# The start of a recurrent kernel: which transfers come first, what TensorE does until they land, and where weight casts and setup stand on VectorE

## What is computed

```python
def step(prev_h, xw_t):
    next_h = jnp.tanh(prev_h @ Wh + xw_t)
    return (next_h, next_h)
...
for e in range(E):
    we = jnp.sum(weights * (indices == e), axis=-1)
    h = jax.nn.silu(x2 @ W1[e].T + b1[e]) * (x2 @ W3[e].T + b3[e])
    y = y + (h @ W2[e].T + b2[e]) * we[:, None]
```

## Time and profile before

| | us |
|---|---|
| median of 3 runs | 152.13 |
| lowest and highest run | 150.54, 154.54 |
| the profiled execution: its own time | 150.08 |
| the profiled execution: its span | 148.3 |
| TensorE busy in the span | 140.9 (95%) |
| VectorE busy | 106.2 (72%) |
| ScalarE busy | 82.7 (56%) |
| GpSimd busy | 32.8 (22%) |

### The profile page before, as it was taken

How to read it: one execution, slowest core, us unless ns; L and a number is a source line. 1 busy time by engine, 2 the same in 40 slices (tenths; PEclk the granted TensorE clock), 3 DMA queues, 4 the chain that set the end, 5 groups by cost and what they waited for, 6 DMA issues and landing times.

```text
span 148.3 us, 3567 instructions
## 1 busy us (share of the span) xinstructions
PE 140.9 (95%) x1126; PEld 131.8 (89%) x1131; DVE 106.2 (72%) x400; ACT 82.7 (56%) x277; POOL 32.8 (22%) x86
## 2 busy tenths in 40 slices
PE   6499999999999999999989999999999999999993
PEld 1368899999899999999979999999999987999892
DVE  4008967698679168645989854999985799969851
ACT  3012247578567337554556554559878812856982
POOL 3003329621469123000016000003321000401100
PEclk9999999999999999999999999999999999999999
DMA  2999200000743000029300009700004910000011
GB/s 50 329 403 396 106 4 0 0 4 13 279 166 119 4 2 0 4 75 343 155 0 4 2 4 290 277 3 0 0 4 144 401 48 0 4 0 18 7 53 53
DMA packets 6834, 13.96 MB, mean 94 GB/s; under 512 B 1600, under 2 KB 3360, under 8 KB 6432
## 3 DMA queue, kind: packets, MB, share of 16 engines
q1 hardware_dynamic: 6384, 13.61, 25.4%
q10 hardware_dynamic: 432, 0.14, 0.4%
HBM read 13.15 MB, written 0.59 MB: 93 GB/s over the span
## 4 chain that ended last, share of the span: by engine, by line
PE 71%; DMA 12%; DVE 10%; issue 4%; ACTq 1%; ACT 1%; DVEq 1%
PE a L1056 15%; PE b L1056 13%; PE y_ps L1167 12%; PE rnn L1099 7%; PE y_ps L1068 6%; DVE hid L986 6%; DMA we_bc<-we_dram 5%; DMA wh_sb<-Wh 4%; DMA we_dram<-weT 3%; PE y_ps L1072 3%; PE b L1167 3%; PE m_ps L1099 2%; DVE hid L977 2%; PE a L1194 2%; PE rnn L1173 1%
## 5 line engine op out<-in xcount | busy, mean ns | idle before, releaser
L977 DVE SCALAR_TENSOR_TENSOR hid<-b,b_sb,gate_u 128x256 f32<-128x256 f32 (+1 forms) x80 | 33.6, 427 | 14.4 <-PE b L1056 10.7
L747 ACT ACTIVATE hs<-rnn 128x8 f32<-128x8 f32 x112 | 19.9, 178 | 33.4 <-PE rnn L1099 31.4
L1099 PEld LDWEIGHTS rnn<-hs,wh_sb 128*128 128x128 f32 x224 | 34.8, 191 | 0.7
L771 ACT ACTIVATE gate_u<-a,b_sb 128x256 f32<-128x256 f32 (+1 forms) x80 | 33.3, 427 | 1.9 <-DVE hid L977 1.0
L1099 PE MATMUL rnn<-hs,wh_sb 128*128 128x8 f32 x224 | 32.6, 218 | 0.0
L1167 PE MATMUL y_ps<-hid,w_sb 128*128 128x128 f32 (+1 forms) x160 | 32.3, 322 | 0.1
L986 DVE TENSOR_TENSOR hid<-hid,we_bc 128x128 f32<-128x128 f32 (+1 forms) x80 | 24.9, 352 | 3.1 <-DMA we_bc<-we_dram 3.1
L1167 PEld LDWEIGHTS y_ps<-hid,w_sb 128*128 128x128 f32 x160 | 24.3, 191 | 1.1
L1056 PE MATMUL a<-hs_hi,w_lo 128*128 128x256 f32 x48 | 16.2, 338 | 0.0
L1056 PE MATMUL a<-hs_hi,w_hi 128*128 128x256 f32 x48 | 15.3, 319 | 0.0
L1056 PE MATMUL a<-hs_lo,w_hi 128*128 128x256 f32 x48 | 15.0, 314 | 0.0
(11 more groups left out here) (152 smaller groups left out, 269.3 us busy)
## 6 DMA issues: line engine op xcount, KB each, us to landing
we_bc<-we_dram SPq DMA_DIRECT2D x12, 512.0 KB, 5.4
we_bc<-we_dram SPq DMA_DIRECT2D x8, 256.0 KB, 3.8
w_sb<-W1T SPq DMA_DIRECT2D x1, 1024.0 KB, 7.3
w_sb<-W3T SPq DMA_DIRECT2D x1, 1024.0 KB, 9.6
w_sb<-W2T SPq DMA_DIRECT2D x1, 1024.0 KB, 7.5
out<-out_sb SPq DMA_DIRECT2D x8, 64.0 KB, 1.5
xT_sb<-xT SPq DMA_DIRECT2D x1, 448.0 KB, 5.2
f_sb<-F1T SPq DMA_DIRECT2D x1, 256.0 KB, 6.9
```

The source lines that it names most:

```text
L747: act.activation(hs[:, cols], rnn_bank(n * BATCH, BATCH), ACT.Tanh).then_inc(h_ready, 1)
L771: act.activation(gate_u[:, n % U_RING, 0:w], a_ps[n % 2][:, 0:w], ACT.Silu, bias=b1_sb[:, e:e + 1]).then_inc(silu_ready, 1)
L977: dve.scalar_tensor_tensor(out=hid[:, n % H_RING, 0:w], in0=b_ps[n % 2][:, 0:w], scalar=b3_sb[:, e:e + 1], in1=gate_u[:, n % U_RING, 0:w], ...
L1099: pe.matmul(rnn_bank(n * BATCH, BATCH), wh_sb[:], prev, start=False, stop=True, skip_group_check=True).then_inc(z_ready, 1)
```

## The change

It does four things.

1. Transfers. The first tile of x moves from the SP queue to the head of ScalarE's queue, `Wh` from the third place there to the second on SP. The bias is loaded as one row of 512 bytes, not as 128 copies of it, and its product contracts over one partition with a row of ones. It is done before the wait for x and `Wx`.
2. TensorE's start. Six wide products of zeros stand ahead of the first wait in place of three, the twelve WARM products between the first steps are gone, and KEEPs of 256 columns may stand there. The one-column bias product moves from behind step 3 to the start.
3. VectorE. The casts may begin only behind step 22 and the setup only behind step 26.
4. The constants of the timetable: assumed landing times, slips, the order in which engines are asked, and `LIFT`. These change the order everywhere.

```diff
-START_KEEPS = 3
-WARM_STEPS = 6
+START_KEEPS = 6
+SPLITS_FROM, SETUP_FROM = 22, 26
...
-RNN_START = 4.7
-PE_SLIP, ACT_SLIP, KEEP_SLIP, MARGIN = 0.3, 0, 0.08, 0.14
+RNN_START = 5.0
+PE_SLIP, ACT_SLIP, KEEP_SLIP, MARGIN = 0.27, 0, 0.09, 0.13
...
-    for kind, t in (("X_IN", 7.2), ("MOE_IN", 12.3), ("L1_IN", 15.4), ("DOWN_IN", 18.0), ("START", RNN_START)):
+    for kind, t in (("SEEDS", 4.8), ("X_IN", 8.0), ("MOE_IN", 12.5), ("L1_IN", 18.0), ("DOWN_IN", 21.0), ("START", RNN_START)):
         put("DMA", kind, 0, 0.0, t)
     for b in range(2):
-        put("DVE", "SEED", b, 0.61, 0.75, [("BIAS", 0)])
+        put("DVE", "SEED", b, 0.61, 0.75, [("SEEDS", 0)])
     quarters = EXPERTS * P // BANK
     for q in range(quarters):
-        put("DVE", "W3_HI", q, 0.34, 0.48, [("MOE_IN", 0)], same("W3_HI", q))
-        put("DVE", "W1_HI", q, 0.34, 0.48, [("MOE_IN", 0)], same("W1_HI", q))
+        put("DVE", "W3_HI", q, 0.34, 0.48, [("MOE_IN", 0)], same("W3_HI", q) + [("TANH", SPLITS_FROM)])
+        put("DVE", "W1_HI", q, 0.34, 0.48, [("MOE_IN", 0)], same("W1_HI", q) + [("TANH", SPLITS_FROM)])
...
-        after = [("SETUP", d - 1)] if d else [("L1_IN", 0)]
+        after = [("SETUP", d - 1)] if d else [("L1_IN", 0), ("TANH", SETUP_FROM)]
...
-            sp.dma_start(xT_sb[:, 0:P], xT[:, 0:P]).then_inc(xw_in, 16)
             sp.dma_start(wx_sb[:], Wx).then_inc(xw_in, 16)
+            sp.dma_start(wh_sb[:], Wh).then_inc(rnn_in, 16)
             sp.dma_start(xT_sb[:, P:TOKENS], xT[:, P:TOKENS]).then_inc(x_in, 16)
...
-            act.dma_start(bh_bc[:], bh.broadcast_to([P, P])).then_inc(xw_in, 16)
+            act.dma_start(xT_sb[:, 0:P], xT[:, 0:P]).then_inc(xw_in, 16)
+            act.dma_start(bh_row[:], bh).then_inc(bias_row_in, 16)
             act.dma_start(h0_sb[:], h0T).then_inc(rnn_in, 16)
-            act.dma_start(wh_sb[:], Wh).then_inc(rnn_in, 16)
...
-            pe.wait_ge(xw_in, 48)
-            pe.wait_ge(row_ready, 1)
+            pe.wait_ge(ones_ready, 1)
+            pe.wait_ge(bias_row_in, 16)
+            pe.matmul(a_ps[0][:, 0:1], bh_row[:], ones_row[:, 0:1], start=True, stop=True, skip_group_check=True).then_inc(marked, 1)
+            pe.matmul(rnn_bank(0, P), bh_row[:], ones_row[:], start=True, stop=False, skip_group_check=True)
+            pe.wait_ge(xw_in, 32)
             rnn_inputs(0)
-            pe.matmul(rnn_bank(0, P), bh_bc[:], first_row[:], start=False, stop=False, skip_group_check=True)
```

More of the change, by code:

```diff
@@ L176, in run @@
         ready = dict.fromkeys(self.ops, 0.0)
-        engines = ("PE", "ACT", "DVE", "POOL", "SP", "DMA")
+        engines = ("PE", "ACT", "POOL", "DVE", "SP", "DMA")
         able = {e: [] for e in engines}
@@ L186, in run @@
         table, rnn_on = "silu", True
-        port, warm = 0.0, False
+        port = 0.0
         a_next, a_free, silu_end = 0, math.inf, {}
@@ L230, in run @@
                     y_idle = y_free is not None and y_free <= t
-                    if e == "PE" and warm and (y_idle or a_next < JOBS and a_free <= t) and (hot is None or t + LOAD < hot + KEEP_SLIP):
+                    if e == "PE" and (y_idle or a_next < JOBS and a_free <= t) and (hot is None or t + LOAD < hot + KEEP_SLIP):
                         orders[e].append(("KEEP", holds) if y_idle else ("KEEP_A", a_next))
@@ L287, in build_orders @@
     same = lambda kind, n: [(kind, n - 1)] if n else []
-    for kind, t in (("X_IN", 7.2), ("MOE_IN", 12.3), ("L1_IN", 15.4), ("DOWN_IN", 18.0), ("START", RNN_START)):
+    for kind, t in (("SEEDS", 4.8), ("X_IN", 8.0), ("MOE_IN", 12.5), ("L1_IN", 18.0), ("DOWN_IN", 21.0), ("START", RNN_START)):
         put("DMA", kind, 0, 0.0, t)
     for b in range(2):
-        put("DVE", "SEED", b, 0.61, 0.75, [("BIAS", 0)])
+        put("DVE", "SEED", b, 0.61, 0.75, [("SEEDS", 0)])
     quarters = EXPERTS * P // BANK
     for q in range(quarters):
-        put("DVE", "W3_HI", q, 0.34, 0.48, [("MOE_IN", 0)], same("W3_HI", q))
-        put("DVE", "W1_HI", q, 0.34, 0.48, [("MOE_IN", 0)], same("W1_HI", q))
+        put("DVE", "W3_HI", q, 0.34, 0.48, [("MOE_IN", 0)], same("W3_HI", q) + [("TANH", SPLITS_FROM)])
+        put("DVE", "W1_HI", q, 0.34, 0.48, [("MOE_IN", 0)], same("W1_HI", q) + [("TANH", SPLITS_FROM)])
         put("DVE", "W1_LO", q, 0.60, 0.74, [("W1_HI", q)], same("W1_LO", q))
         put("POOL", "W3_LO", q, 1.23, 1.37, [("W3_HI", q)], same("W3_LO", q))
-    put("PE", "BIAS", 0, [(LOAD, 0.007)] * 2, RESULT, [], [("RNN", WARM_STEPS // 2)])
-    for k in range(2 * WARM_STEPS):
-        put("PE", "WARM", k, [(LOAD, 0.213)], RESULT, [], [("RNN", k // 2)] + same("WARM", k))
     for t in range(STEPS):
         behind = same("RNN", t)
-        if 0 < t <= WARM_STEPS:
-            behind.append(("WARM", 2 * t - 1))
         if t and t % STEPS_PER_TILE == 0:
@@ L472, in adaln_ffn @@
         wx_sb, wh_sb = sb("wx_sb", [P, P]), sb("wh_sb", [P, P])
-        bh_bc, first_row = sb("bh_bc", [P, P]), sb("first_row", [P, P])
+        bh_row, ones_row = sb("bh_row", [1, P]), sb("ones_row", [1, P])
         hs = sb("hs", [P, TOKENS])
@@ L820, in link @@
                 dve.wait_ge(chain, links[0])
[L823 to L825 removed]
+            dve.memset(ones_row[:], 1.0).then_inc(ones_ready, 1)
             for t in (gmax, g_take):
@@ L992, in _ @@
                         dve.wait_ge(x_in, 16)
-                        dve.wait_ge(xw_in, 48)
+                        dve.wait_ge(xw_in, 32)
                     dve.wait_ge(y_done, (n + 1) * EXPERTS)
@@ L1042, in rnn_inputs @@
             def rnn_inputs(i):
-                pe.matmul(rnn_bank(i * P, P), wx_sb[:], xT_sb[:, tile_cols(i)], start=(i == 0), stop=False,
+                pe.matmul(rnn_bank(i * P, P), wx_sb[:], xT_sb[:, tile_cols(i)], start=False, stop=False,
                           skip_group_check=True)
@@ L1078, in _ @@
                 keep_wide()
-            pe.wait_ge(xw_in, 48)
-            pe.wait_ge(row_ready, 1)
+            pe.wait_ge(ones_ready, 1)
[3 more added lines that the diff above has]
+            pe.wait_ge(xw_in, 32)
             rnn_inputs(0)
-            pe.matmul(rnn_bank(0, P), bh_bc[:], first_row[:], start=False, stop=False, skip_group_check=True)
             for kind, n in ORDERS["PE"]:
-                if kind == "WARM":
-                    keep_wide()
-                if kind == "BIAS":
-                    pe.matmul(a_ps[0][:, 0:1], bh_bc[:], first_row[:, 0:1], start=True, stop=True, skip_group_check=True).then_inc(marked, 1)
                 if kind == "XIN":
```

12 lines of the change are left out of this document (4 added, 8 removed), and 8 rows, old and new, of the table LIFT.

## The result

The changed kernel took 145.91 us (median of four executions, 145.71 to 146.02). The kernel before took 153.13 us (four executions, 150.54 to 154.54). The ratio is 0.964, with a 95% interval from 0.955 to 0.973: 3.6% faster. The profiled executions are 145.98 and 150.08 us, with spans of 144.2 and 148.3.

What follows compares the result with a forecast made beforehand. It took TensorE's queued work, and when that may begin with the recurrence, as the bound. Start -2.3, middle -0.3 and tail +0.5 made -2.1 us, from the median 152.13 to 150.0 us, range 147.6 to 152.4.

Steps and rivals of the forecast that it cites:

- the casts fit beside the `hid`: VectorE, 20 to 53 us: 28.0 of 33 us busy, one cast of 0.36 us a step beside one `hid`.
- the tail costs 0.5 us more: Behind step 64: four fewer passes of A and B done by the last step, at 0.127 us each, +0.5 us.
- The wait of 39.80: Weighting at 39.19 waited 0.94 us for weights, TensorE stood 0.32; to go, with the slow copy at 26.04, for -0.7.
- one collision with a subtraction: VectorE's copy of `dT` at 26.04 took 1.22 us beside a GpSimd subtraction; to go, one new wait of +0.4 expected.
- -0.3 forecast for steps 16 to 64: Middle stretch: two old waits go, -0.7, and one new wait beside GpSimd's subtractions comes, +0.4.
- the casts stop the experts: VectorE, steps 22 to 46: each cast takes 0.89 us and delays a `hid`, 3.9 us lost, 153.5 us; chance 0.1.
- The clock: TensorE's start: rise at 6.9 us, only step 0 at the low level, 1.7 of 2.0 lost us come back.
- the first rival: TensorE's start: clock rises by 5.5, step 0 at 5.7, step 16 at 16.3, total -3.5, 148.6 us; chance 0.32.
- a rival: TensorE's start: clock rises late, four steps at about 1.1 us, sum -0.6 to -0.1, about 151.7 us; chance 0.18.
- My -2.3 for the start: Start to step 16: step 0 at 6.5 us and an earlier clock rise put step 16 at 17.3, not 19.6.
- The landing: First transfers: `Wh` lands at 5.56 us, `h0` at 6.1 with bounds 6.1 to 7.0; step 0 gains 0.6 us.
- The distance to the median: Whole kernel: the profiled 150.08 lay 2.05 us under the median 152.13; this distance was carried over to the changed kernel.

Runs made afterwards that it cites:

- the eight profiles: Profiles of the change, its variants and the kernel before with the new start, all with six wide products and early transfers; tanh of step 16 at 16.9 to 20.5 us.
- the run with ten zeros: Kernel before with the new start, plus ten narrow products of zeros between the inputs and step 0: 152.22 us, ratio 1.011.

## Why the prediction was off

**Right.** The end is set by when TensorE's full stretch begins; the casts fit beside the `hid` (0.41 us, one 0.71); the tail costs 0.5 us more. The wait of 39.80 went, because the weights are asked for 9 us earlier, and one collision with a subtraction went and another came: -0.3 forecast for steps 16 to 64, -0.6 measured. The slower rival, "the casts stop the experts", is refuted by VectorE at 28.34 of 33 us with TensorE at 32.91.

**The clock, by 0.6 us.** The step that failed was "with the 5.6 us that the rise took before, it comes at 6.9". It was there before 5.1 in the first profile. That took 0.4 off the products ahead of step 0 and the 0.2 of a step at the lower level, and with the landing below step 16 began at 16.47, not 17.3. That is nearer to the first rival (16.3; span 3.5 us less forecast, 4.1 measured). But no value was right for all: four of the eight profiles have the rise before 5.5, the others between about 10 and 13. I read a duration off one execution and used it as a property of the kernel. The Trainium skill's sentence on its variation stood in my text, and I gave it to a rival instead of to the width of my own case. My -2.3 for the start lies near the average difference of 2.2, and that is luck: no profile has the rise where I put it.

**The landing, by 0.2 us.** I put `Wh` at 5.56 and `h0` at 6.1. `Wh` landed at 3.8 (1.16 and 2.6), `h0` at 5.8. Both bounds of `h0` were too late in this execution; in others it landed up to 1.3 us later, at 7.2, beyond my upper bound of 7.0. I took `h0`'s time from its own place in the queue; it follows the big transfer of x, as the last section shows.

**Steps 64 to 127, -0.9 us.** I had no term there. The wait was to be seen at 74.74, and I had looked no further than step 64. It comes and goes with the landing of one chunk's weights.

**The distance to the median, 2.1 us.** This is the largest. I carried over the 2.05 us by which the profiled execution lay under the median, as if it were a constant of the program. For the changed kernel it is -0.07 in the first timing (145.98 profiled, median 145.91) and 1.4 us the other way in the second (149.79 profiled, median 148.39). The profile that I had read, of 150.08 us, was faster than any of the four timed executions, with step 16 at 20.0 where two later profiles of that start have 22.1: a rise that comes late makes 2.1 us by itself. The wait at 39.19, which I priced at the 0.32 us of one execution, can cost 15, but none of the four executions that make the 153.13 is over 154.54, so such a loss is in none of them. How much of the 2.1 each of the two gave stays open. Term by term: 0.8 (start) + 0.3 (16 to 64) + 0.9 (64 to 127) make the 2.0 us between the forecast span of 146.2 and 144.2, and 2.1 more make the 4.1.

**Luck in the measurement.** The four executions of the first timing lie within 0.3 us of each other and of the profiled one, which had the early rise; that all four had it is likely and not shown. The second timing gave 148.39, which is 1.6 us below the forecast and inside the range. There the forecast would have looked right, with the same wrong steps in it.

## What to carry to other kernels

A wait of TensorE in the middle of a full stretch is not worth only its length: it is a chance for the clock to fall. So look first at the other engine's queue: move the instruction that waits for a late operand further back, so that nothing that TensorE needs stands behind it. If the runs of a kernel spread by several per cent, ask which wait makes the long ones before you carry the distance from profile to median over to a change. A gain that hangs on the clock's rise at the start has to be timed more than once, and profiled more than once: here the two medians were 145.9 and 148.4, and the single times behind the second 146.1 to 149.8. Before you explain a loss by the edit you made, look for the stretch in which it stands: the run with ten zeros at the start lost its time near 94 us.

## What the runs showed of the hardware

- **A small transfer lands with the big one.** `h0` (4 KB, issued at 1.72) and the 448 KB of x (issued at 1.63) took, in the ten profiles with this order of issue: 4.1 and 4.0 us twice, 4.5 and 4.4, 4.5 and 4.5, 4.6 and 4.6, 4.8 and 4.7, 5.0 and 4.9, 5.2 and 5.1, 5.3 and 5.2, 5.4 and 5.3. Step 0 waits for `h0`, so the big transfer sets when it can begin. In the order of before `Wh` stood in that place, issued 0.01 us behind the big one: in the four profiles with it, it landed 0.16 to 0.18 us behind it (7.05 and 6.87 in the first). Moved ahead of it, it landed 2.1 to 2.6 us after its issue. The Trainium skill, "DMA: Bandwidth & Descriptors", section "Queues, rings and completion order", says that a semaphore's increment lands only after every earlier write of that DMA engine, across its queues; these pairs agree. That this rule is the reason isn't shown: `h0` ahead of x in the queues wasn't tried.
- **The first rise isn't in the clock's column.** From 1.0 to 12.6 us of the second profile of the change the granted clock reads 1.00, while products take twice as long; the falls at 7.2 us (0.54) and at 41 us (0.50) are in it.
- **Where the clock fell.** In these profiles it fell behind waits of 0.85, 1.25, 1.56, 1.59 and 1.92 us, 0.5 to 1.7 us after their ends or, once, 0.1 us before (the 1.56). It didn't behind those of 0.63 us and less that stood at the high level.
- **A full TensorE didn't bring the clock back at once**: 26.00 of 26.00 us busy at a granted clock of 0.50, behind a pause of 1.56 us. Behind the pause of 1.59 us in the run with ten zeros it was back after 3.4 us. Why it stayed so much longer in the one is open.
